# Where VectorE's side work stands in the second half of a two-batch cross attention

## What is computed

```
x = x + _L0_xattn_ref(_layernorm(x), ctx_2048, Wq, Wk, Wv, Wo)      # 16 heads of 128, 2048 keys
x = x + _L0_attn_ref(_layernorm(x), W_in, b_in, ...)                # "mix"
x = x + _L0_ffn_ref(_layernorm(x), gate_w, expert_w, expert_b)      # "experts", top 2 of 8
x = x + _L1_xattn_ref(_layernorm(x), ctx_2048, Wq, Wkv, ...)        # 16 heads of 16, fake-quantized q, k, v
x = x + _L1_attn_ref(_layernorm(x))
x = x + _L1_ffn_ref(_layernorm(x), w_gate, w_up, w_down)            # weights and activations quantized in blocks of 32
...
v = _fq_sym(v, axis=2)        # one scale for each of 256 columns: s = max|v| / 127; v is rounded to v * (1 / s)
...
q = _quantize_elem(xb / scale, ebits, mfrac, max_norm) * scale      # per block of 32: power-of-two unit, round, cut to the limits
```

## Time and profile before

| | us |
|---|---|
| median of 3 runs | 711.92 |
| lowest, highest | 711.22, 712.50 |
| the profiled execution, its time | 711.99 |
| its span in the profile | 710.7 |

### The profile page before, as it was taken

How to read it: one execution, slowest core, us unless ns; L and a number is a source line. 1 busy time by engine, 2 the same in 40 slices (tenths; PEclk the granted TensorE clock), 3 DMA queues, 4 the chain that set the end, 5 groups by cost and what they waited for, 6 DMA issues and landing times. The chain is left out here.

```text
span 710.7 us, 13245 instructions
## 1 busy us (share of the span) xinstructions
PE 663.2 (93%) x4895; PEld 421.4 (59%) x4895; DVE 553.9 (78%) x1000; ACT 379.9 (53%) x610; POOL 334.9 (47%) x449
## 2 busy tenths in 40 slices
PE   8899999999999979999999998988999789987887
PEld 6467666676666756766776765763446334443453
DVE  5997877976877777688898665658997889988655
ACT  5633433344333434354453344418989799898841
POOL 5884545445454432576664133517645443344401
PEclk9999999999999999999999999999999999999999
DMA  9657788565566668989656738629998989898910
GB/s 308 180 119 161 160 172 184 128 143 131 131 137 144 130 150 214 200 195 196 144 150 159 168 77 176 138 56 261 204 187 144 174 150 191 154 178 156 165 38 8
DMA packets 347152, 111.23 MB, mean 157 GB/s; under 512 B 313544, under 2 KB 344528, under 8 KB 346832
## 3 DMA queue, kind: packets, MB, share of 16 engines
q1 hardware_dynamic: 347088, 110.39, 73.7%
HBM read 32.23 MB, written 0.26 MB: 46 GB/s over the span
## 5 line engine op out<-in xcount | busy, mean ns | idle before, releaser
L910 PE MATMUL psum<-c_nat,eT 128*128 128x256 f16 x1536 | 189.2, 274 | 1.1 <-ACT u_sb L1041 1.1
L1644 DVE TENSOR_REDUCE tops<-psum 128x1 f32<-128x512 f32 x256 | 158.7, 682 | 20.2 <-PE psum L1628 19.9
L910 PEld LDWEIGHTS psum<-c_nat,eT 128*128 128x128 f16 x1536 | 151.0, 98 | 27.3 <-issue 1.8
L882 PE MATMUL psum<-cT,qk 128*128 128x512 f16 x744 | 165.6, 379 | 0.1
L1719 ACT ACTIVATE cT<-psum,bias,q_scale 128x1024 f16<-128x1024 f32 x128 | 153.5, 1205 | 17.1 <-PE psum L1628 12.8
L1628 PE MATMUL psum<-kT,v_space 128*128 128x512 f16 x512 | 139.1, 380 | 16.6 <-DVE tops L1644 9.7
L882 PEld LDWEIGHTS psum<-cT,qk 128*128 128x128 f16 x744 | 72.7, 98 | 82.1 <-issue 1.0
L1078 DVE TENSOR_REDUCE neg_max<-psum 128x1 f32<-128x2048 f32 x32 | 73.2, 2289 | 31.5 <-PE psum L882 31.2
L1628 PEld LDWEIGHTS psum<-kT,v_space 128*128 128x128 f16 x512 | 44.2, 97 | 82.0 <-DVE tops L1644 46.0
L1066 DVE TENSOR_TENSOR e_lo<-e_all,e_hi 128x2048 f16<-128x2048 f32 x32 | 84.2, 2632 | 0.0
L730 ACT ACTIVATE qT<-psum 128x128 f32<-128x128 f32 x32 | 8.9, 279 | 126.2 <-PE psum L712 126.0
(11 more groups left out here) (252 smaller groups left out, 903.7 us busy)
## 6 DMA issues: line engine op xcount, KB each, us to landing
wq_h<-in_L_xattn_Wq SPq DMA_DIRECT2D x32, 128.0 KB, 2.4
wk_h<-in_wkT SPq DMA_DIRECT2D x32, 128.0 KB, 2.6
wv_h<-in_L_xattn_Wv SPq DMA_DIRECT2D x32, 128.0 KB, 2.3
wo_h<-in_L_xattn_Wo SPq DMA_DIRECT2D x32, 128.0 KB, 2.5
mx_land<-in_mx_weights SPq DMA_DIRECT2D x8, 384.0 KB, 3.7
v_space<-in_ctx SPq DMA_DIRECT2D x4, 512.0 KB, 6.0
cT<-in_ctx SPq DMA_DIRECT2D x2, 1024.0 KB, 8.4
c_nat<-in_expert_wT SPq DMA_DIRECT2D x2, 1024.0 KB, 7.1
```

The costliest lines, as they stand in the source:

```text
L882: ins = pe.matmul(s_ps[:, n * 512:(n + 1) * 512], c.qk[:, u % 2, q_part, k, :], m.cT[:, b, c_part, 4 * n:4 * n + 4, k, :], start=(k, q_par ...
L910: ins = pe.matmul(u_ps, c.eT[:, v % 2, e_part, j, :], m.c_nat[:, v // H0, c_part, j, :], start=(j, e_part, c_part) == (0, 0, 0), stop=(j, ...
L1644: dve.tensor_reduce(m.tops[:, n // NB, n % NB:n % NB + 1], m.bank(n % 3), AX.X, ALU.max, negate=True).then_inc(s["q_max"], 1)
```

## The change

In `dve_cross` the slice work (units or cut) and the side work change places around two instructions. Before, a step from 16 on was: side work of slot 4u, the slice work, side work of slot 4u+1, the output added to x, `qk_lo`, side work of slot 4u+2. After, it is: side work of slots 4u and 4u+1, the output added to x, side work of slot 4u+2, `qk_lo`, the slice work. The product of ones and diagonals moves on PE from step 17 to step 18, and the copy of its result on DVE from the end of `dve_value_scales` to a function of its own, called in step 18. Nothing is added or left out.

```diff
@@ pe_cross
+        if u == H0 + 2:
+            pe.wait_ge(s["v_scale_dve"], V_SCALE_DVE["diag1"])
+            pe.matmul(kv_ps[:, 0:D], m.ones[:, :], g.diagonals[:, :], start=True, stop=True).then_inc(
+                s["v_scale_pe"], 1)
         if 0 <= v < UNITS:
             attend(v, 0)
...
-        if u == H0 + 1:
-            pe.wait_ge(s["v_scale_dve"], V_SCALE_DVE["diag1"])
-            pe.matmul(kv_ps[:, 0:D], m.ones[:, :], g.diagonals[:, :], start=True, stop=True).then_inc(
-                s["v_scale_pe"], 1)
@@ dve_cross
-        side.upto(4 * u)
-        n = (u - H0) // 2
-        if H0 <= u < UNITS and (u - H0) % 2 == 0:
-            dve_slice_units(dve, g, s, n)
-        elif H0 <= u < UNITS:
-            dve_slice_cut(dve, g, s, n)
         side.upto(4 * u + 1)
         drain(u, 0)
         if w is not None:
             add_output(w)
         if u < H0:
             dve_key_tile(dve, m, d, s, 2 * u + 1)
+        side.upto(4 * u + 2)
         if u + 2 < UNITS:
             dve_fold_key(dve, m, c, s, u + 2)
-        side.upto(4 * u + 2)
+        if u == H0 + 2:
+            dve_value_inverses(dve, m, s, kv_ps)
+        n = (u - H0) // 2
+        if H0 <= u < UNITS and (u - H0) % 2 == 0:
+            dve_slice_units(dve, g, s, n)
+        elif H0 <= u < UNITS:
+            dve_slice_cut(dve, g, s, n)
@@ dve_value_scales
+def dve_value_inverses(dve, m, s, ps):
     dve.wait_ge(s["v_scale_pe"], V_SCALE_PE["inverse"])
     dve.wait_ge(s["scores"], H0)
-    dve.tensor_copy(m.mix["v_inv"], ps[:, 0:D]).then_inc(sem, 1)
+    dve.tensor_copy(m.mix["v_inv"], ps[:, 0:D]).then_inc(s["v_scale_dve"], 1)
```

## The result

| | before | after |
|---|---|---|
| median | 712.21 us (4 runs) | 720.99 us (4 runs) |
| lowest, highest | 711.22, 712.63 | 720.11, 722.06 |
| profiled execution: time, span | 711.99, 710.7 | 721.19, 719.9 |

The account below looks back on a forecast made before the run. PE was taken to set the pace, with only 8.7 us of waits to win. 711.99 + 0.0 (to unit 22's scores) + 0.0 (steps 22 to 28) + 0.8 (step 30) = 712.8, stated as 712.7 us; range 709.0 to 716.0.

Parts of the forecast that it names:

- What bounds the kernel: Steps 18 to 29: PE sets the pace; only its waits, together 8.7 us, can be won.
- Steps 16 and 17: PE's waits of 2.14 and 2.58 us go, a new one of 2.0 us comes; gain 3.5 us.
- S(18): Start of the scores of unit 18 in PE's order (other units likewise); forecast 264.9, before 268.36.
- Steps 17 to 21: The early gain is given back: late SP transpose and the cut behind `qk_lo` make PE wait 3.8 us in step 20.
- S(21): Start of the scores of unit 21 on PE; forecast 306.2, 1.3 us later than before.
- rival (2): PE's clock drops behind the new wait of step 20, costing 1.8 us: 714.5 us; chance 0.20.
- S(22): Start of the scores of unit 22 on PE; forecast 320.5, where it was before.
- Steps 22 to 28: DVE's six steps take 76 us against PE's 79.6, so DVE keeps up; 0.0 us change.
- rival (3): POOL's rounding slows DVE by 1.6 us in each even step, 2.7 us by step 28: 715.5 us; chance 0.14.
- Step 30: The cut behind `qk_lo` lengthens PE's wait for the normed x from 2.71 to about 3.5 us: + 0.8.
- Rival (1): Transpose of `e_hi` of 18 lands by 291.9 or DVE's cut is quick; early gain stays: 708.8 us; chance 0.26.
- The signs named: Profile marks from step 17 to 30 meant to show whether the forecast or one of three rivals holds.

Follow-up runs that it names:

- The early coefficients: Changed kernel with the gate's six coefficient operations in slot (26,2), ahead of `qk_lo`, instead of (26,3): 716.15 us, ratio 1.0032.
- the missing rounding: Changed kernel with POOL's rounding of each weight slice cut to 1 of its 768 columns, all waits kept: 714.54 us, ratio 1.0012.
- the cut of step 19 ahead: Changed kernel with only the cut of step 19 again ahead of the output and `qk_lo`: 716.05 us, ratio 1.0052.
- the run with the idle products: Changed kernel plus fourteen PE products whose result isn't used, ahead of the scores of unit 21: 721.27 us, ratio 1.0113.
- the product alone: Kernel before, with only the diagonals' product and the copy of its result moved to step 18: 712.40 us, ratio 0.9984.
- the one with only the units behind: Changed kernel with the cuts of odd steps ahead of the output and `qk_lo` as before, units of even steps behind: 708.71 us, ratio 0.9934.
- the best version: Changed kernel with cuts ahead of the output and `qk_lo` as before, units behind, gate coefficients in slot (26,2): 706.16 us, ratio 0.9903.
- the cuts alone: Changed kernel with units of even steps ahead of the output and `qk_lo` as before, only cuts behind: 716.83 us, ratio 1.0050.

## Why the prediction was wrong, step by step

**What bounds the kernel.** Right that PE set the pace and that only waits were to be won, and the point from which `qk_lo` can start holds: 307.77 - 300.98 = 6.8 us. But I counted DVE's loop from undisturbed durations, and left out what POOL does to them.

**Steps 16 and 17: right.** Both waits of step 17 went and one came before S(18): 1.31 us instead of 2.0, since `e_lo` of 16 was no longer stretched (2.28 us instead of 3.45). The gain was 4.15 us, forecast 3.5. The product cost step 18 only 0.43 us (276.83 - 264.21 - 12.19), not 0.70.

**Steps 17 to 21: right in S(21), by two errors that cancel.** S(21) was forecast at 306.2 and came at 305.68, PE's waits as 3.8 us and they were 3.67. But `e_hi` of 19 came at 291.99 and not at 293.95. "SP is 0.85 us late from there on" was wrong: the transpose of `e_lo` of 17 was issued 0.17 us late and stood 0.73 us less in the issue, and SP was early from there. That 291.99 is near the lower bound I had given, 291.9, is chance. I gave it as the time when ACT would be ready; ACT was ready at 289.14 and waited for the landing. And from `qk_lo` to the maximum of 20 DVE took 6.79 us, not 5.44, because the rounding of the values took 1.69 instead of 0.60, beside POOL's own (1.74 us from 296.08), and `e_lo` 2.68 instead of 2.20. Moving the one cut of step 19 or the loads shows that both parts of the sum stood at the right place. POOL's wait in step 21 did go, 1.26 us.

**The clock in step 20: rival (2), true and without effect there.** The scores of 21 were 2.86 us slower, more than the 1.8 I had from the earlier trace rows, and S(22) is therefore 322.67 and not 320.5. I priced this as a loss that stays. With the clock kept up in step 20, S(24) is the same, so this term of rival (2) is nothing at the end of the sum, as long as DVE is the next bound. The low clock behind the wait of step 27, which I had not foreseen, did cost: 1.5 us.

**Steps 22 to 28: the step that failed.** "So DVE keeps up, with 0.6 us a step to spare." DVE's maxima of units 20 to 26 start at 300.98, 315.64, 328.91, 343.58, 356.32, 371.10 and 383.25. The even steps are 14.66, 14.67 and 14.78 us, forecast 13.1; the odd ones 13.27, 12.74 and 12.15, forecast 12.2. Six steps are 82.3 us, forecast 76, and PE has 79.6. The mechanism is rival (3), and its price for the even step was 14.7. What I held against it, that only the end of `e_lo` would be left to overlap, was wrong: POOL's own rounding of the values was long done, and POOL started on the slice at 311.39, 0.44 us ahead of `e_lo`. The odd steps are longer too, as the cut's first pass took 1.98 and 1.53 us in steps 21 and 23 instead of the 0.95 at its best. Without POOL's rounding of the slices the even steps are 13.05, 13.33 and 13.16 us and all six 77.2. So DVE's own rows were summed rightly, and the term put at nothing was POOL's rounding of the slices beside them: 5.1 us in these six steps, where PE's 79.6 had left 3.6.

**Step 26: a term that wasn't in the sum.** "The side work of DVE falls into the 6.8 us and costs nothing there." That holds for slots 4u to 4u+2. Slot 4u+3 stands behind the slice work, and the coefficients are in it. From the trace of before they were 1.2 us (387.15 to 388.32), beside an idle POOL. Now they are 4.63 us, the even step is 17.2 us long, and behind it stands not only the exponential but the expert sum for which PE waits 3.09 us. With the slow product behind it (3.46 us, at full clock 1.98) this is 4.6 of the 4.8 us by which S(27) to S(28) is longer. And the price stood in the trace of before: while POOL rounded at 382.85 and 384.74, an operation of DVE on one column took 1.60 us at 383.08 and one on two columns 1.71 at 384.86. Even without that I should have asked in which slot each item of the tables is. The early coefficients take 6.7 us out of the time (1.0126 against 1.0032), the missing rounding 8.1, the cut of step 19 ahead 5.3. Each of these is a change to the changed kernel, on another chip, and good to about 2 us; they don't add up to the 9 us, since the 4 us won in step 17 can be kept as well.

**Step 30: too dear.** The wait is 2.75 us, forecast 3.5. The chain was counted rightly: from the start of `qk_lo` to that of the normed x it is 449.46 - 442.30 = 7.16 us, where before it was 439.84 - 433.61 = 6.23, 0.9 more. But "that moves with PE" was not exact: ACT's `e_hi` starts 1.35 us behind the scores of 30 (440.10 - 438.75), before 2.09 (431.41 - 429.32), since it is held 4.55 us for the transpose instead of 5.29. With the cut ahead the wait is 1.35 us, so the cut does cost its length here. The slow clock behind this wait in before is absent in after, and S(28) to S(31) is 1.2 us shorter for it.

**Rival (1)** did not hold in the changed kernel, although the landing that it asked for nearly came: 291.99. Its own sum was wrong too: from a landing at 291.9 the prediction's terms give `qk_lo` at 294.1 and, 5.44 us behind, the maximum of 20 at 299.5 and not at 297.5. It started at 300.98, since the rounding and `e_lo` behind the cut were slow. The signs named: SP at 271.29 (forecast 272), ACT until 291.99 (294), DVE idle before 11 of the 13 `qk_lo` from step 17 to 29, clock below 1.00 near 306, S(22) not near 320.5, and S(28) 6.8 us later than S(22) makes it, where rival (3) had 2.

On rival (3) the Trainium skill, "GPSIMD Engine Reference", section "1. Specifications", says that GpSimd contends with VectorE instructions of two SBUF inputs or in a 2-port perf mode. By that rule the result came out on its side; I should have given it more than 0.14. The trace agrees for `e_lo` (3.90 against 2.28), and shows it for small operations too: one on 8 columns took 1.86 us against 0.29. On rival (2), the Trainium skill, "TensorE: Matmul & The Clock Gate", section "HAM oscillation — how this bites in real kernels", says that the burst behind a wait starts slow. It was right on step 20 (8.20 us against 5.34). That this costs nothing where another engine is the next bound, only the run with the idle products shows.

**What stays open.** The last 1.4 us of the 9.2 (from +7.80 at S(31) to +9.2 at the end) come in pieces. By the starts of the same DVE instructions the changed kernel is 8.11 us late at 478 us, 8.48 at 519, 8.50 at 573 and 9.15 at 594 (times of before), and stays so. The step of 0.65 us lies where its clock is low (0.83 from 580 to 590, 0.97 from 550 to 600); the rest was not traced. The clock from 550 to 600 was 1.00 in before, in the run with the product alone and in the one with only the units behind, 0.97 with the changed kernel, the cut of 19 and the best version, 0.93 in the others. What decides it there was not tried.

## What to carry to other kernels

Work moved from ahead of an awaited result to behind it adds its full length to its engine's loop whenever the engine would have been idle ahead of it. So add up the whole loop of that engine, step by step, with the longest duration of each row and not the undisturbed one, and compare pairs of steps with the pace of the bounding engine: 14.7 + 13.3 was too long, 14.7 + 10.1 was not. And of a work order in slots, look up where each slot now stands; one item of six small operations in the wrong slot was over half of this loss (4.8 of 9.2 us). A gap on the engine that sets the pace, the slow clock in step 20 here, is worth nothing by itself when a second loop is as long.

## What the hardware showed that I had not expected

- A small operation of DVE that meets a pass of POOL over 768 columns ends only with that pass. In step 26 one on one column took 1.60 us (0.16 beside an idle POOL) and one on 8 columns 1.86 (0.29); they ended at 395.57 and 397.48, and POOL's passes at 395.57 and 397.45. The large `e_lo` goes from 2.28 to 3.90. Not every one is held: a reciprocal at 393.77, 0.01 us behind the start of POOL's pass, took 0.17.
- The length of PE's wait alone does not tell whether the clock falls. The wait of 3.09 us in step 27 was followed by a product of 3.46 us in the changed kernel and of 1.98 us, full speed, in two experiments. A wait of 2.32 before the scores of 24 was followed by 7.03 us for them in one and by 5.34 in two others. In step 17 twelve products took 1.47 us behind a wait of 2.14 (before) and 2.70 and 2.72 behind waits of 2.17 and 2.12 (the product alone, the cuts alone). A wait of 3.67, 3.48 or 3.31 before the scores of 21 was always followed by slow ones (four kernels), one of 3.07 was not. I have no rule for the shorter ones.
- Of DVE's `e_lo` and POOL's rounding of a slice the one that starts while the other runs is the one that is held up. In the changed kernel `e_lo` is 0.16 us ahead in steps 16, 28 and 30: 2.28 us, and POOL's pass 3.79 instead of 1.81. In steps 20, 22 and 24 POOL is 0.44 us ahead: 3.89 or 3.90 us, and POOL's pass 2.19. No run changed only the order.
- A transpose that SP issues behind a row of thirteen loads stands in the issue for 5.35 us, and the next one goes out when it has left (288.99). With six of the loads taken from ahead of it, it was issued 4.3 us earlier and still stood there 4.54 us.
